# Hyperbolic attention: sums of ratio and root by accumulating DMAs that GpSimd issues, six pairs of heads instead of four through products

## The chip, the cores and the metric

The kernel runs on one NeuronCore of a Trainium2 chip. Its engines are TensorE (PE; its weight loads are shown apart as PEld), VectorE (DVE), ScalarE (ACT), GpSimd (POOL) and SyncE (SP), which run their own instruction streams in order and meet at semaphores, and 16 DMA engines. The metric is the device time of one execution in microseconds (us). A profiled execution is described by its span, from the first to the last instruction.

## The reference, cut to what matters

The program computes two transformer blocks on `x` of 32 x 256 x 128 (32 batches of 256 tokens of width 128, float32): causal attention, a mixture of experts, hyperbolic attention, and an MLP, each on a layer-normed input and with a residual. The change touches the third part alone:

```python
def _hyperbolic_distance(q, k, c):                      # c = 1, 16 heads of width 8
    q_norm_sq = jnp.sum(q * q, axis=-1, keepdims=True)
    k_norm_sq = jnp.sum(k * k, axis=-1)[..., None, :]
    qk = jnp.einsum('bhnd,bhmd->bhnm', q, k)
    diff_sq = q_norm_sq + k_norm_sq - 2.0 * qk
    denom = (1.0 - c * q_norm_sq) * (1.0 - c * k_norm_sq)
    denom = jnp.maximum(denom, 1e-06)
    cosh_arg = 1.0 + 2.0 * c * diff_sq / denom
    cosh_arg = jnp.maximum(cosh_arg, 1.0)
    return jnp.arccosh(cosh_arg)
...
attn = jax.nn.softmax(-dist, axis=-1)
out = jnp.einsum('bhnm,bhmd->bhnd', attn, v)
```

With s = cosh_arg - 1, the weight before normalising is exp(-arccosh(1+s)) = 1 / (1 + s + sqrt(s(s+2))). The same number is 1 / (sqrt(1+s/2) + sqrt(s/2))^2. The kernel uses the first form for some heads and the second for the others.

## The kernel before, in words

Four stages follow each other: `causal_attention`, `moe`, `hyperbolic_attention` (L1235 on) and `mlp`. The hyperbolic stage lies between about 1300 and 2425 us of the span. It works batch by batch (`b` = 0 to 31), and within a batch by 8 pairs of heads (`p` = 0 to 7). One pair is a tile of 128 partitions x 1024 float32 (two heads, two halves of 128 query rows, 256 keys), so 4 KB in each partition and 512 KB in all.

A pair of batch `b` goes this way:

- PE multiplies feature rows into `d_ps` and `i_ps` in PSUM (`pe_pairs`, L1353). There is one buffer of each, so the multiplies of the next pair wait until DVE has read `d_ps` (`dist_done`) and `i_ps` (`u_done`).
- DVE makes u = max(d, 0) (`dve_distances`, L1528) and then u = min(i, 1e6) * u (`dve_ratio`, L1532), the ratio s. `u` is a ring of 12 tiles (RING), and a slot is free again when PE has multiplied the weights that were in it with the values (`pv_done`).
- For the pairs in PRODUCTS (0, 1, 2, 3) GpSimd computes s(s+2) into one of six `spare` tiles (`pool_product`, three instructions, L1468, L1469, L1471). ACT takes one root of it in place (L1433). For the pairs 4 to 7 ACT takes two roots itself (`act_roots`): sqrt(1+s/2) into `spare` (L1438) and sqrt(s/2) in place in `u` (L1439).
- GpSimd adds `spare` to `u` (`pool_sum`, L1460).
- ACT takes the logarithm of the sum and the exponential of its multiple (`act_weights`, L1447 and L1450).
- PE multiplies the weights with the values (`pe_values`, L1369). Transposes, a normalisation on DVE (L1544, L1547), a projection and a residual follow.

The order on each engine is written out by hand. ACT does, in the loop body of batch `b`, the logarithms and exponentials of batch `b - 1`, and then the roots of batch `b`, with a load of its function table ahead of each of the two groups (L1654 and L1433). GpSimd does the products of batch `b` and then its eight sums, nothing else. DVE does ratios and distances of batch `b` with the row features of batch `b + 1` (`dve_features`, in the turn of pair 4), the copies of transposed rows (L1426), and the normalising of batch `b - 2` between them. PE follows the same pairs.

`spare` has six tiles (SPARE) for eight pairs: pair `p` uses tile `p % 6`. `spare_user` names who had the tile before: pair 6 of batch `b - 1` for pair 0, pair 7 of batch `b - 1` for pair 1, the same pair of batch `b - 1` for the pairs 2 to 5, and pairs 0 and 1 of the same batch for the pairs 6 and 7. Whoever writes `spare` waits until that sum is finished (`sum_done`).

Of the kernel before, what the change touches and what calls it, by code (L numbers as in the profile page):

```python
# [12 lines left out]
ALU = mybir.AluOpType  # L13
# [38 lines left out]
def after(engine, semaphore, count):  # L52

    if isinstance(count, int) and count <= 0:
        return
    engine.wait_ge(semaphore, count)
# [303 lines left out]
def causal_attention(nc, keep, batches):  # L360
# [12 lines left out]
    with ExitStack() as stack:  # L373
# [99 lines left out]
        def pe_turn(pe, p, s):  # L473
            k = p * SLOTS + s
            pe.wait_ge(exp_done, k + 1)
            wait_turned(pe, *at_lag(p, s, 2))
            for c in range(4):
                last = nc.tensor.transpose(t_ps[s % 2][:, c * P:(c + 1) * P], prob[:, s % 3, c, :], keep.ident)  # L478
            last.then_inc(p_turned, 1)

        def pe_values(pe, p, u, i):
            g, a = divmod(u, 2)
            wait_turned(pe, p, 3 * u)
            wait_turned(pe, p, 3 * u + 2)
            if a == 0:
                after(pe, o_copied, p * GROUPS + g)
                if g == 0:
                    pe.wait_ge(v_done, p + 1)
                    pe.wait_ge(v_cleared, 2)
            for q in range(GH):  # L490
                nc.tensor.matmul(o_ps[q * ROWS:(q + 1) * ROWS, a * N:(a + 1) * N], v[:, i, a * TB, g * GH + q, :],
                                 pT[:, u % 2, q, 0:2, :], start=True, stop=False, skip_group_check=True)
            for q in range(GH):
                last = nc.tensor.matmul(o_ps[q * ROWS:(q + 1) * ROWS, a * N + P:(a + 1) * N],
                                        v[:, i, a * TB + 1, g * GH + q, :], pT[:, u % 2, q, 2, :], start=False,
                                        stop=True, skip_group_check=True)
            last.then_inc(pv_done, 1)

        def pe_turn_back(pe, p, t, makes):
            pe.wait_ge(o_copied, (p + 1) * GROUPS)  # L500
            pe.wait_ge(v_done, makes)
            after(pe, attn_done, p * PT + t)
            for g in range(GROUPS):
                last = nc.tensor.transpose(misc[:, g * P:(g + 1) * P], o[:, t // TB, g, t % TB * P:(t % TB + 1) * P],
                                           keep.ident)
            last.then_inc(o_turned, 1)

        def pe_turn_attn(pe, p):
            pe.wait_ge(attn_done, (p + 1) * PT)
            for t in range(PT):  # L510
                last = nc.tensor.transpose(misc[:, t * P:(t + 1) * P], attn[:, t, :], keep.ident)
            last.then_inc(attn_turned, 1)
# [152 lines left out]

        END = pairs - 1

        with nc.Block() as block:
            @block.tensor
            def _(pe):  # L670
# [31 lines left out]
                for s in range(SLOTS - TURN_LAG, SLOTS):  # L702
                    pe_turn(pe, END, s)
                for u in range(UNITS - 2, UNITS):
                    pe_values(pe, END, u, 1)
                for t in range(PT):
                    pe_turn_back(pe, END, t, pairs)
                pe_turn_attn(pe, END)
                pe_project(pe, END)

# [527 lines left out]
def hyperbolic_attention(nc, keep, batches):  # L1238
# [3 lines left out]
    HP = H // 2  # L1242
# [5 lines left out]
    SPARE = 6  # L1248
    RING = 12
    TURN = 3  # L1250
    PRODUCTS = (0, 1, 2, 3)
    ROWS_BY_SCALAR = (0, 3)
    EARLY_ROWS = 5
    VALUES_AT = (2, 3, 4, 5)
# [1 line left out]
    with ExitStack() as stack:  # L1256
# [8 lines left out]
        u = m.sb("u", [P, RING, 2 * W2])  # L1265
        spare = m.sb("spare", [P, SPARE, 2 * W2])
# [21 lines left out]
        S_ = m.sem  # L1288
# [6 lines left out]
        inv_hi_done, rows_done, rows_turned, rowsT_done = S_("inv_hi_done"), S_("rows_done"), S_("rows_turned"), [S_(f"rowsT_done{n}") for n in range(2)]  # L1295
        pair_ready, dist_done, u_done = S_("pair_ready"), S_("dist_done"), S_("u_done")
        raised = S_("raised")
        prod_done, root_done, sum_done, ln_done, w_done, pv_done = S_("prod_done"), S_("root_done"), S_("sum_done3"), S_("ln_done"), S_("w_done"), S_("pv_done3")
        o_copied, o_turned, rec_done, attn_done = S_("o_copied3"), S_("o_turned3"), S_("rec_done3"), S_("attn_done3")
        attn_turned, attnT_done, proj_ready, res_done = S_("attn_turned3"), S_("attnT_done3"), S_("proj_ready3"), S_("res_done3")  # L1300

        def spare_user(b, p):

            return (b, p - SPARE) if p >= SPARE else (b - 1, p + SPARE if p + SPARE < HP else p)

        def slot(i, p):

            return (i * HP + p) % RING
# [120 lines left out]
        def act_roots(act, b, p, i):  # L1429
            pair, extra = u[:, slot(i, p), :], spare[:, p % SPARE, :]  # L1430
            if p in PRODUCTS:
                act.wait_ge(prod_done, b * len(PRODUCTS) + PRODUCTS.index(p) + 1)
                last = nc.scalar.activation(extra, extra, ACT.Sqrt)  # L1433
            else:
                act.wait_ge(u_done, b * HP + p + 1)
                before = spare_user(b, p)
                after(act, sum_done, before[0] * HP + before[1] + 1)
                nc.scalar.activation(extra, pair, ACT.Sqrt, bias=1.0, scale=0.5)  # L1438
                last = nc.scalar.activation(pair, pair, ACT.Sqrt, scale=0.5)  # L1439
            last.then_inc(root_done, 1)  # L1440

        def act_weights(act, b, p, i, logarithm):
            pair = u[:, slot(i, p), :]
            whole = p in PRODUCTS
            if logarithm:
                act.wait_ge(sum_done, b * HP + p + 1)
                nc.scalar.activation(pair, pair, ACT.Ln, bias=1.0 if whole else 0.0).then_inc(ln_done, 1)  # L1447
            else:
                act.wait_ge(ln_done, b * HP + p + 1)
                nc.scalar.activation(pair, pair, ACT.Exp, scale=-1.0 if whole else -2.0).then_inc(w_done, 1)  # L1450
# [6 lines left out]

        def pool_sum(pool, b, p, i):
            pool.wait_ge(root_done, b * HP + p + 1)
            nc.gpsimd.tensor_tensor(u[:, slot(i, p), :], u[:, slot(i, p), :], spare[:, p % SPARE, :], ALU.add).then_inc(sum_done, 1)  # L1460

        def pool_product(pool, b, p, i):
            pool.wait_ge(u_done, b * HP + p + 1)
            before = spare_user(b, p)
            after(pool, sum_done, before[0] * HP + before[1] + 1)
            n = b * len(PRODUCTS) + PRODUCTS.index(p)
            pair, extra = u[:, slot(i, p), :], spare[:, p % SPARE, :]
            nc.gpsimd.tensor_tensor(extra[:, 0:4], pair[:, 0:4], twos[:, :], ALU.add)  # L1468
            nc.gpsimd.tensor_scalar(extra[:, 4:2 * W2], pair[:, 4:2 * W2], 1.0, 2.0, ALU.mult, ALU.add).then_inc(raised, 1)  # L1469
            pool.wait_ge(raised, n + 1)  # L1470
            nc.gpsimd.tensor_tensor(extra, extra, pair, ALU.mult).then_inc(prod_done, 1)  # L1471
# [96 lines left out]
        def over_batches(engine, body):  # L1568


            def turn(r, some):
                for i in range(some):
                    b = TURN * r + i
                    known = isinstance(b, int)
                    body(b, i, not known or b >= 1, not known or b >= 2, not known or b >= 3, not known or b + 1 < batches,
                         not known or b + 2 < batches)
            whole = batches // TURN
            turn(0, TURN)
            with engine.Fori(1, whole) as r:
                turn(r, TURN)  # L1580
            turn(whole, batches % TURN)

        END = batches - 1

        with nc.Block() as block:
# [92 lines left out]
            @block.gpsimd  # L1678
            def _(pool):
                nc.gpsimd.memset(rows[:, :, :, :, :].bitcast(F32), 0.0).then_inc(v_cleared, 1)  # L1680
                nc.gpsimd.memset(v[:, :, :, :, DH:ROWS], 0.0).then_inc(v_cleared, 1)
                pool.wait_ge(v_cleared, 2)
                nc.gpsimd.memset(rows[:, 0, :, :, NORM_K:NORM_K + 2].bitcast(F32), 1.0).then_inc(zeroed, 1)
                nc.gpsimd.memset(rows[:, 1, :, :, NORM_Q:NORM_Q + 2].bitcast(F32), 1.0).then_inc(zeroed, 1)
                nc.gpsimd.memset(v[:, :, :, :, DH:VW], 1.0).then_inc(zeroed, 2)
                nc.gpsimd.memset(twos[:, :], 2.0).then_inc(v_cleared, 1)
                pool.wait_ge(v_cleared, 3)

                def body(b, i, one_before, two_before, three_before, one_after, two_after):
                    for p in PRODUCTS:  # L1690
                        pool_product(pool, b, p, i)
                    for p in range(HP):
                        pool_sum(pool, b, p, i)
                over_batches(pool, body)

            @block.vector
            def _(dve):
# [296 lines left out]
```

## Time and profile before

| | |
|---|---|
| median of 3 runs | 2583.7 us (2578.2 to 2590.47) |
| span of the profiled execution | 2563.6 us |
| median less span (what lies around the instructions) | 20.1 us |
| hyperbolic stage | about 1300 to 2425 us |
| PE, DVE, ACT, POOL busy over the span | 81%, 78%, 72%, 65% |

The shares over the whole span say little, because the four stages have different limits. Within the hyperbolic stage the work repeats once for each batch, so it is read as a period: the time between one event and the same event of the next batch. For an engine, busy time in a stretch, idle time before an instruction, and who ended that idle time are the three things to look for. An engine can be busy for nearly the whole period and still not set it, if the little idle time it has is a wait for somebody else. The time of an instruction is from its start to its end; back to back instructions overlap a little, so the distance from start to start is the pace.

### The profile page before, as it was taken

The page shows a single profiled execution, that of the slowest core. Times are in us where ns is not written, and L with a number is a line of the kernel's source. Part 1 is how long each engine was busy: PE and PEld are TensorE (multiplying, and loading weights), DVE is VectorE, ACT ScalarE, POOL GpSimd, SP SyncE. Part 2 cuts the span into 40 slices and gives each one's busy share as a digit, 9 for nine tenths or more (in the row PEclk, how much of TensorE's full clock was granted, in tenths as well). Part 3 has the DMA queues.
Part 4 walks back from the last instruction along what each step waited for, and adds up shares of the span by engine and source line. Part 5 has one row for each costly group of instructions (what it writes and reads, how often), then busy time and mean ns, then how long its engine had stood idle before and what let it go on. Part 6 is the DMA issues. An engine that isn't in the chain of part 4 may idle for free. (4 is left out here: it accounts for less than half of the span.)

```text
span 2563.6 us, 50172 instructions
## 1 busy us (share of the span) xinstructions
PE 2079.1 (81%) x14935; PEld 1515.9 (59%) x14935; DVE 1998.1 (78%) x6007; ACT 1854.7 (72%) x3188; POOL 1663.5 (65%) x1516
## 2 busy tenths in 40 slices
PE   4999999999999979999947666666666666666599
PEld 4777777777777668888834444443433444434266
DVE  4677777777777757877768999999999999999522
ACT  2666666666666634344239999999999999999743
POOL 2767766676667400000058999999999999999600
PEclk7999999999999969999966677777777777777599
DMA  5000000000000024334200000000000000000011
GB/s 136 1 2 2 1 1 0 1 0 1 1 0 1 2 67 108 93 92 110 68 1 1 1 1 0 0 0 0 0 0 0 0 0 0 0 0 1 7 31 37
DMA packets 44067, 49.03 MB, mean 19 GB/s; under 512 B 5112, under 2 KB 27038, under 8 KB 43934
## 3 DMA queue, kind: packets, MB, share of 16 engines
q1 hardware_dynamic: 35614, 43.32, 7.0%
q10 hardware_dynamic: 8320, 4.19, 0.7%
q8 instruction: 52, 0.85, 0.1%
q14 instruction: 81, 0.66, 0.1%
HBM read 42.78 MB, written 4.72 MB: 19 GB/s over the span
## 5 line engine op out<-in xcount | busy, mean ns | idle before, releaser
L1460 POOL TENSOR_TENSOR u<-u,spare 128x1024 f32<-128x1024 f32 x256 | 597.2, 2372 | 35.1 <-ACT spare L1433 34.9
L545 ACT ACTIVATE prob<-s_ps,nmax 128x128 f32<-128x128 f32 (+1 forms) x1024 | 364.4, 432 | 140.1 <-DVE nmax L602 140.0
L1353 PE MATMUL d_ps<-rowsT 28*128 28x256 f32 x1024 | 165.9, 404 | 331.3 <-DVE u L1532 331.2
L602 DVE CUSTOM_DVE_ANT_0 s_ps<-s_ps,mask 128x128 f32<-128x128 f32 (+1 forms) x1024 | 341.3, 385 | 101.8 <-issue 77.9
L1353 PEld LDWEIGHTS d_ps<-rowsT 28*128 28x128 f32 x1024 | 106.2, 242 | 430.4 <-issue 430.0
L582 POOL TENSOR_TENSOR g_lo<-g_all,g_hi 128x512 fp32r<-128x512 f32 x256 | 329.1, 1286 | 21.4
L1528 DVE TENSOR_SCALAR u<-d_ps 128x1024 f32<-128x1024 f32 x256 | 311.9, 1218 | 39.5 <-PE i_ps L1353 39.3
L1532 DVE SCALAR_TENSOR_TENSOR u<-i_ps,u 128x1024 f32<-128x1024 f32 x256 | 313.5, 1225 | 14.8
L1471 POOL TENSOR_TENSOR spare<-spare,u 128x1024 f32<-128x1024 f32 x128 | 303.1, 2368 | 10.7
L1447 ACT ACTIVATE u<-u 128x1024 f32<-128x1024 f32 x256 | 258.3, 1070 | 0.0
L1450 ACT ACTIVATE u<-u 128x1024 f32<-128x1024 f32 x256 | 257.5, 1066 | 0.0
L537 ACT COPY g_all<-g_ps 128x512 f32<-128x512 f32 x256 | 151.6, 592 | 126.9 <-PE g_ps L63 125.9
L994 POOL TENSOR_TENSOR x_lo<-xTs,x_hi 128x512 fp32r<-128x512 f32 x16 | 21.9, 1366 | 327.0 <-ACT x_hi L990 327.0
L1369 PE MATMUL o_ps<-u,v 128*32 128x256 f32 x2048 | 197.8, 522 | 43.1 <-ACT u L1450 43.0
L478 PE MATMUL t_ps<-ident,prob 128*128 128x128 f32 x1536 | 229.8, 272 | 1.6 <-ACT pT L612 1.2
L1341 PE MATMUL r_ps<-ident,rows 128*128 128x128 f32 x1024 | 217.9, 360 | 6.8 <-DVE rows L1523 6.1
L478 PEld LDWEIGHTS t_ps<-ident,prob 128*128 128x128 f32 x1536 | 190.6, 140 | 54.8 <-ACT prob L545 2.0
L1162 ACT ACTIVATE act_g<-eg_ps 128x512 f32<-128x512 f32 x128 | 76.3, 598 | 189.9 <-PE eg_ps L63 188.1
L1341 PEld LDWEIGHTS r_ps<-ident,rows 128*128 128x128 f32 x1024 | 163.9, 186 | 69.3 <-issue 53.5
L615 DVE COPY pT<-t_ps 128x512 f32<-128x512 f32 x256 | 176.7, 690 | 28.5 <-PE t_ps L478 22.6
L61 PE MATMUL s_ps<-g_hi,x_hi 128*128 128x512 f32 x384 | 185.9, 484 | 3.8 <-POOL g_lo L582 3.8
L558 POOL TENSOR_TENSOR g_hi<-g_all,ones 128x4 fp32r<-128x4 f32 x256 | 51.5, 201 | 194.6 <-ACT g_all L537 191.1
(265 smaller groups left out, 5577.9 us busy)
## 6 DMA issues: line engine op xcount, KB each, us to landing
w_all<-w_rows SPq DMA_DIRECT2D x128, 256.0 KB, 5.6
x<-L_attn_x ACTq DMA_DIRECT2D x8, 512.0 KB, 14.0
y<-y_rows SPq DMA_DIRECT2D x16, 256.0 KB, 2.3
wkqv<-L_attn_Wkqv SPq DMA_DIRECT2D x4, 528.0 KB, 8.7
gate_rows<-L_ffn_gate_proj SPq DMA_DIRECT2D x1, 512.0 KB, 14.5
up_rows<-L_ffn_up_proj SPq DMA_DIRECT2D x1, 512.0 KB, 11.5
down_cols<-L_ffn_down_proj SPq DMA_DIRECT2D x1, 512.0 KB, 13.3
w_rows<-wT SPq DMA_DIRECT2D x8, 64.0 KB, 1.6
```

The lines of the kernel that those rows point to most:

```text
L478: last = nc.tensor.transpose(t_ps[s % 2][:, c * P:(c + 1) * P], prob[:, s % 3, c, :], keep.ident)
L545: last = nc.scalar.activation(prob[:, kind, at, :].rearrange("p c n -> p (c n)"), s_ps[kind][:, at.start * P:at.stop * P], ACT.Exp, bias=n ...
L582: nc.gpsimd.tensor_tensor(g_lo[:, gb, q, :], g_all[:, h % 2, :], g_hi[:, gb, q, :], ALU.subtract).then_inc(g_split, 1)
L602: last = nc.vector.tensor_tensor_reduce(out=scores, in0=scores, in1=keep.mask[:, N - width:N], scale=-1.0, scalar=3.4e38, op0=ALU.add, op1 ...
L1341: last = nc.tensor.transpose(r_ps[p % 2][:, at:at + P], src, keep.ident)
L1353: last = nc.tensor.matmul(ps[:, e * W2 + j * N:e * W2 + (j + 1) * N], rowsT[at, slot(i, p), 1, j * P:(j + 1) * P], rowsT[at, slot(i, p), 0 ...
L1447: nc.scalar.activation(pair, pair, ACT.Ln, bias=1.0 if whole else 0.0).then_inc(ln_done, 1)
L1450: nc.scalar.activation(pair, pair, ACT.Exp, scale=-1.0 if whole else -2.0).then_inc(w_done, 1)
L1460: nc.gpsimd.tensor_tensor(u[:, slot(i, p), :], u[:, slot(i, p), :], spare[:, p % SPARE, :], ALU.add).then_inc(sum_done, 1)
L1471: nc.gpsimd.tensor_tensor(extra, extra, pair, ALU.mult).then_inc(prod_done, 1)
L1528: nc.vector.tensor_scalar(u[:, slot(i, p), :], d_ps[:, :], 0.0, None, ALU.max).then_inc(dist_done, 1)
L1532: nc.vector.scalar_tensor_tensor(out=u[:, slot(i, p), :], in0=i_ps[:, :], scalar=1.0 / DEN_MIN, in1=u[:, slot(i, p), :], op0=ALU.min, op1= ...
```

## The change

`pool_sum` no longer adds on GpSimd. It issues a DMA from `spare` to the pair's tile of `u` that adds to what is there (`accum_op=ALU.add`). Each of the six tiles of `spare` has a semaphore of its own (`sum_landed`) that this DMA raises by 16 when it has landed. Everybody who waited for `sum_done` now waits for it through `wait_sum`: ACT ahead of a logarithm, and ACT or GpSimd ahead of writing `spare`. PRODUCTS becomes (0, 1, 2, 3, 4, 5): the pairs 4 and 5 get three GpSimd instructions each, and ACT takes one root for them instead of two. The loop of GpSimd over the batches is written out, so that its waits are for constants, and it waits for the last eight sums at its end.

```diff
-    PRODUCTS = (0, 1, 2, 3)
+    PRODUCTS = (0, 1, 2, 3, 4, 5)
...
+        sum_landed = [S_(f"sum_landed{n}") for n in range(SPARE)]
...
+        def wait_sum(engine, b, p):
+
+            users = 2 if p % SPARE < HP - SPARE else 1
+            after(engine, sum_landed[p % SPARE], 16 * (users * b + p // SPARE + 1))
...
                 act.wait_ge(u_done, b * HP + p + 1)
-                before = spare_user(b, p)
-                after(act, sum_done, before[0] * HP + before[1] + 1)
+                wait_sum(act, *spare_user(b, p))
...
             if logarithm:
-                act.wait_ge(sum_done, b * HP + p + 1)
+                wait_sum(act, b, p)
...
         def pool_sum(pool, b, p, i):
             pool.wait_ge(root_done, b * HP + p + 1)
-            nc.gpsimd.tensor_tensor(u[:, slot(i, p), :], u[:, slot(i, p), :], spare[:, p % SPARE, :], ALU.add).then_inc(sum_done, 1)
+            nc.gpsimd.dma_start(u[:, slot(i, p), :], spare[:, p % SPARE, :], accum_op=ALU.add).then_inc(sum_landed[p % SPARE], 16)
 
         def pool_product(pool, b, p, i):
             pool.wait_ge(u_done, b * HP + p + 1)
-            before = spare_user(b, p)
-            after(pool, sum_done, before[0] * HP + before[1] + 1)
+            wait_sum(pool, *spare_user(b, p))
...
+        def written_out(body):
+
+            for b in range(batches):
+                body(b, b % TURN, b >= 1, b >= 2, b >= 3, b + 1 < batches, b + 2 < batches)
...
-                over_batches(pool, body)
+                written_out(body)
+                for p in range(HP):
+                    wait_sum(pool, END, p)
```

On GpSimd, at the boundary of batch 0 and batch 1, the kernel before has the last product of a batch, its eight sums, and the first product of the next batch in this order:

```order
L1468 TENSOR_TENSOR spare<-u,twos 128x4 [waits u_done]
L1469 TENSOR_SCALAR spare<-u 128x1020
L1471 TENSOR_TENSOR spare<-spare,u 128x1024 [waits raised]
L1460 TENSOR_TENSOR u<-u,spare 128x1024 [waits root_done] x8
L1468 TENSOR_TENSOR spare<-u,twos 128x4 [waits sum_done3,u_done]
```

The same place (last product of batch 1, its sums, first products of batch 2) in the changed kernel:

```order
L1472 TENSOR_TENSOR spare<-u,twos 128x4 [waits sum_landed5,u_done]
L1473 TENSOR_SCALAR spare<-u 128x1020
L1475 TENSOR_TENSOR spare<-spare,u 128x1024 [waits raised]
L1465 DMA u<-spare 128x1024 [waits root_done] x8
L1472 TENSOR_TENSOR spare<-u,twos 128x4 [waits sum_landed0,u_done]
L1473 TENSOR_SCALAR spare<-u 128x1020
L1475 TENSOR_TENSOR spare<-spare,u 128x1024 [waits raised]
L1472 TENSOR_TENSOR spare<-u,twos 128x4 [waits sum_landed1,u_done]
```

Eight sums are now eight issues, and the first products behind them wait for the landing of the sums of the pairs 6 (`sum_landed0`) and 7 (`sum_landed1`) of the batch ahead. The additions themselves have left the engine's stream, so its order no longer fulfils that wait.

On ACT, the roots of a batch stand in the kernel before behind the table load like this:

```order
L1433 ACT_TABLE_LOAD
L1433 ACTIVATE spare<-spare 128x1024 [waits prod_done] x4
L1438 ACTIVATE spare<-u 128x1024 [waits sum_done3,u_done]
L1439 ACTIVATE u<-u 128x1024
L1426 CAST rowsT<-r_ps 128x512 [waits pair_ready,rows_turned]
```

and in the changed kernel like this:

```order
L1439 ACT_TABLE_LOAD
L1439 ACTIVATE spare<-spare 128x1024 [waits prod_done] x5
L1432 CAST rowsT<-r_ps 128x512 [waits pair_ready,rows_turned]
L1439 ACTIVATE spare<-spare 128x1024 [waits prod_done]
L1443 ACTIVATE spare<-u 128x1024 [waits sum_landed0,u_done]
L1444 ACTIVATE u<-u 128x1024
L1443 ACTIVATE spare<-u 128x1024 [waits sum_landed1,u_done]
L1444 ACTIVATE u<-u 128x1024
```

Two of the four double roots have become single ones, and the two that remain (pairs 6 and 7) wait for the landing of the sums of the pairs 0 and 1 of the same batch.

## Rows read from the trace of the kernel before

**Rows 1.** Busy us of each engine by stretch, then PE clock, DMA share, GB/s.
```profile
core 0: us, PE busy (x) PEld busy (x) DVE busy (x) ACT busy (x) POOL busy (x), PEclk, DMA share, GB/s
1700.00:1800.00 100.00, 64.74 (x534) 40.50 (x538) 91.40 (x177) 97.47 (x125) 95.98 (x60) 0.72 0.00 0
```

**Rows 2.** Waits between 1500 and 2100 us: total us, times, longest us.
```profile
PE d_ps L1353 <- DVE u L1532: 186.3, 105, 4.9
PE o_ps L1369 <- ACT u L1450: 21.4, 18, 1.2
DVE rec L1544 <- PE misc L1380: 21.2, 18, 1.2
POOL u L1460 <- ACT spare L1433: 18.3, 18, 1.2
DVE u L1528 <- PE i_ps L1353: 17.5, 35, 0.5
ACT rows L1417 <- PE r_ps L1341: 13.6, 17, 0.9
```

**Rows 3.** Timeline of PE: start us, us, engine, line, operation [idle before <-releaser].
```profile
1739.07 1.07 PE L1369 MATMUL o_ps<-u,v 128*32 128x256 f32 x16 [1.23 <-ACT u L1450]
1740.08 0.83 PE L1380 MATMUL misc<-ident,o 128*128 128x128 f32 x4
1745.43 0.58 PE L1353 MATMUL d_ps<-rowsT 28*128 28x256 f32 x2 [4.52 <-DVE u L1532]
```

**Rows 4.** Timeline of ACT: the table load of batches five and thirty.
```profile
1484.26 1.28 ACT L1654 ACT_TABLE_LOAD   x1
...
2337.74 1.28 ACT L1654 ACT_TABLE_LOAD   x1
```

**Rows 5.** Timeline of ACT, the roots of a batch.
```profile
1709.33 1.28 ACT L1433 ACT_TABLE_LOAD   x1
1710.62 3.90 ACT L1433 ACTIVATE spare<-spare 128x1024 f32<-128x1024 f32 x4
1714.43 1.04 ACT L1438 ACTIVATE spare<-u 128x1024 f32<-128x1024 f32 x1
1715.38 1.04 ACT L1439 ACTIVATE u<-u 128x1024 f32<-128x1024 f32 x1
```

**Rows 6.** Timeline of POOL: a batch's last product, its sums, two products behind them.
```profile
1707.15 0.21 POOL L1468 TENSOR_TENSOR spare<-u,twos 128x4 f32<-128x4 f32 x1
...
1711.76 18.66 POOL L1460 TENSOR_TENSOR u<-u,spare 128x1024 f32<-128x1024 f32 x8 [0.97 <-ACT spare L1433]
1730.36 0.22 POOL L1468 TENSOR_TENSOR spare<-u,twos 128x4 f32<-128x4 f32 x1
...
1734.00 0.20 POOL L1468 TENSOR_TENSOR spare<-u,twos 128x4 f32<-128x4 f32 x1
```

**Rows 7.** Busy time by stretch, as in rows 1, where DMAs run.
```profile
10.00:12.00 2.00, 1.11 (x5) 1.11 (x6) 0.18 (x1) 0.00 (x0) 0.00 (x0) 1.00 1.11 332
950.00:1000.00 50.00, 50.00 (x314) 43.28 (x313) 39.45 (x109) 22.37 (x42) 2.60 (x2) 1.00 0.36 87
```

**Rows 8.** DMA issues: tile, queue, operation, times, KB each, median us to landing.
```profile
y<-y_rows SPq DMA_DIRECT2D x16, 256.0 KB, 2.3
w_rows<-wT SPq DMA_DIRECT2D x8, 64.0 KB, 1.6
```

**Rows 9.** Timeline of SyncE's queue: start us, us that one issue takes.
```profile
2449.48 0.39 SPq L1888 DMA_DIRECT2D y<-y_rows  x1
```

**Rows 10.** Timeline of POOL, the first batch: its first product and its first sum.
```profile
1316.44 0.20 POOL L1468 TENSOR_TENSOR spare<-u,twos 128x4 f32<-128x4 f32 x1 [17.83 <-DVE u L1532]
...
1330.84 18.59 POOL L1460 TENSOR_TENSOR u<-u,spare 128x1024 f32<-128x1024 f32 x8
```

**Rows 11.** Timeline of ACT, the last batch: its first root and its last logarithms.
```profile
2389.12 2.96 ACT L1433 ACTIVATE spare<-spare 128x1024 f32<-128x1024 f32 x3
...
2416.75 1.99 ACT L1447 ACTIVATE u<-u 128x1024 f32<-128x1024 f32 x2
```

More of the change, by code:

```diff
@@ L1297, in hyperbolic_attention @@
         raised = S_("raised")
-        prod_done, root_done, sum_done, ln_done, w_done, pv_done = S_("prod_done"), S_("root_done"), S_("sum_done3"), S_("ln_done"), S_("w_done"), S_("pv_done3")
+        prod_done, root_done, ln_done, w_done, pv_done = S_("prod_done"), S_("root_done"), S_("ln_done"), S_("w_done"), S_("pv_done3")
+        sum_landed = [S_(f"sum_landed{n}") for n in range(SPARE)]
         o_copied, o_turned, rec_done, attn_done = S_("o_copied3"), S_("o_turned3"), S_("rec_done3"), S_("attn_done3")
```

## The prediction

> **What bounds the kernel now.** I read the busy time by stretch first, then the waits, then the timelines. In a stretch of the hyperbolic stage the DMA share is 0.00 while ACT is busy 97%, POOL 96% and DVE 91% [rows 1]. By shares, ACT or POOL seem to set the pace, and the change relieves both. The waits say otherwise [rows 2]. The stretch of 600 us holds some 18 batches. POOL idles 1.0 us a batch, ahead of its first sum, for ACT. ACT idles 0.8 us a batch, for PE's transposes of feature rows. DVE idles for PE alone: 1.2 us a batch ahead of the normalising and twice 0.5 us ahead of a distance. No row has DVE waiting for ACT or POOL. PE waits for DVE, 10 us a batch. PE waits for ACT too, 1.2 us a batch, but that wait is covered: it stands at 1739.07, the work behind it is over at 1740.9, and then PE idles 4.52 us more until DVE frees the single PSUM buffers [rows 3]. So the period is a loop of DVE and PE, and ACT and POOL follow it with about 1 us to spare. The period is (2337.74 - 1484.26) / 25 = 34.14 us [rows 4].
>
> **What the change removes.** On POOL eight sums of 18.66 us in all [rows 6]. On ACT two of the eight L1438/L1439 roots of a batch, one start to start distance of 0.95 us each [rows 5], 1.9 us. Both engines only have slack before the loop of DVE and PE, so this takes nothing from the period. What is late next is what was late before: DVE.
>
> **What it adds on POOL.** A product costs the distance between two of them, 1734.00 - 1730.36 = 3.6 us [rows 6], so two more cost 7.2 and six cost 21.7. Then there are eight issues. The trace has no DMA issued by POOL. The nearest row is SyncE's issue, 0.39 us [rows 9]; the other end is the 2.33 us of the sum it replaces, since a reason to be dearer than the addition of 1024 elements is not in sight. I take 1.0, about the geometric mean of the two. POOL's own work is then 21.7 + 8.0 = 29.7 us of 34.14. POOL is not too busy.
>
> **What it adds in DMA.** Eight transfers of 512 KB per batch, where nothing moved. No row shows an accumulating DMA, so I bound its pace T. One pass over 524288 bytes at 332 GB/s, the best rate of a stretch [rows 7], is 1.58 us. But an addition has to read both `spare` and `u`, so twice that many bytes come in for each tile written: 3.16 us. A slower row is the copies of weights, 87 GB/s at a share of 0.36, so 242 GB/s if the engines were always busy [rows 7]; two reads at that pace are 4.33 us. I take 3.16: two reads are what the operation needs, and the 332 was reached with the engines saturated (share 1.11), as they will be here. For starting and completing I take the store of 64 KB, 1.6 us to landing less 0.2 for its bytes, and the one of 256 KB, 2.3 less 0.8 [rows 8]: 1.5 us, with 1.0 to 3 as bounds.
>
> The Trainium skill, Collectives: The Full Stack, section The bandwidth ceiling: the fold count and why AG ≠ RS ≠ AR, says of an adding DMA that it is slower than a copy because it reads two sources through one ring, not because of the add, with some 31 GB/s per DMA engine for the reading. The estimate from that page is 16 x 31 / 2 = 248 GB/s, T = 2.1; the period formed below would be 39.0 and the time about 2735. No row here shows an adding DMA.
>
> **The new wait, and the chain behind it.** GpSimd executes in order: products of a batch, issues of its sums, products of the next batch. The first two products of the next batch write the `spare` tiles of the pairs 6 and 7. They used to find these sums done, because POOL had just done them itself. Now POOL stands there until the DMAs have landed, and the four products behind them stand too. Those are waited for by ACT's roots, and the roots by the next issues. With E the end of a batch's sixth product, the loop is:
> - issue of the first sum: 1.0. Its root is long done, and the roots of the pairs 1 to 5 come at 0.95 us each or are done, faster than T. The roots of 6 and 7 wait for sums 0 and 1 to land, but are issued while sums 2 to 5 still move.
> - start and completion: 1.5.
> - seven sums until that of pair 6 has landed: 7 x 3.16 = 22.1. The sum of pair 7 lands during the first product, which is longer (3.6).
> - six products: 21.7.
>
> Sum: 46.3 us from E to E. It exceeds 34.14, so it becomes the period, and DVE, ACT and PE wait for it. For T over 3.6 the last sum decides instead: 2.5 + 8T + 18.1.
>
> **The sum.** In the first batch the products begin at 1316.44 [rows 10], so the sixth ends at 1316.44 + 21.7 = 1338.1. After 31 periods the sixth product of the last batch ends at 1338.1 + 31 x 46.3 = 2773.4. Eight sums land 1.0 + 1.5 + 25.3 = 27.8 later, at 2801.2, and the last logarithms start. Before, they start at 2416.75 [rows 11]. The rest behind them is unchanged, so the span grows by 384 us, from 2563.6 to 2948. That is the profiled execution's own measure; with the 20 us by which the median of the runs stands above it, it is 2968, my forecast. The PE clock, 0.72 here [rows 1], does not matter: PE is not in the chain. Nor is the logarithm of the pairs 4 and 5, which takes the other form at the same price.
>
> **The rivals.**
> *Two reads, but quicker.* The 332 GB/s came from loads of the inputs from HBM; here source and target are both tiles on the core, with rows of 4 KB. With T = 2.36, halfway between one pass and two, the period is 2.5 + 16.5 + 21.7 = 40.7, and the same steps give about 2790. Chance 0.25 for T between 1.6 and 2.7 (2620 to 2870).
> *Slower adding.* T of 4.33 gives 2.5 + 34.6 + 18.1 = 55.2, 653 us for 31 periods and some 20 more at the ends: 3257. T could be more if the adding limits. Chance 0.18 for T over 3.9 (over 3150).
> *One pass.* If reading the second operand costs nothing, T = 1.58: 2.5 + 11.1 + 21.7 = 35.3, so 1.1 x 31 = 35 us more, about 2620. With the cheap ends (issue 0.4, start and end 1.0) it is 34.2 and the loop of DVE and PE keeps the pace: 2584. Chance 0.07 together with the next one, 0.05 of it within 0.5%.
> *A plain copy's pace.* A quicker transfer, under 1.5, leaves POOL with slack and the change does nothing, 2584. The Trainium skill, DMA: Bandwidth & Descriptors, section Anatomy of one DMA, gives 2.0 us and bytes at 436 GB/s for a DMA from GpSimd, so 1.2 us a tile; its figures are for copies, and the estimate by it is a period of 1.0 + 2.0 + 8.4 + 21.7 = 33.1, no change. This trace never reaches that rate.
> *Faster.* If the 0.8 us that ACT waits a batch is an effect and ACT is what really closes the loop with PE (PE waits 1.2 us for its weights), then 1.9 us less on ACT shorten every period, provided T is under about 1.4, from where six products and eight landings fit into 32.2 us. It gives 2583.7 - 60 = 2524. Against it: 4.5 us of idle time behind that wait [rows 3]. Chance 0.05.
>
> **How the numbers follow.** Forecast (T of 2.7 to 3.9) 0.45, quicker 0.25, slower adding 0.18, one pass or copy's pace 0.07, faster 0.05. The range goes from 2600, just under one pass with its likely prices, to 3300, just over two reads at the slowest row; about 0.08 lies above and 0.10 below. Half a per cent (13 us) is about what can be told from no change. Faster by more: 0.05. Within: 0.05. Slower by more: 0.90.
>
> **What would show it.** In the changed profile POOL's first product of each batch (L1472) should be preceded by some 13 us of idle time (24.6 us from E to the landing of the sum of pair 6, less the 12 us until the last issue) that a DMA ended; DMAs should be busy over half of the period; ACT should wait ahead of the roots of pair 6 (L1443) and for the products (L1439). DVE's share should fall from 91% to some 67%. A table load should come every 46 us. I am wrong in T if landings are spaced otherwise than 3.16 us, in the cost of an issue if POOL's issues follow at more than 1 us, and in the whole chain if POOL doesn't idle. If the period is 34 with idle POOL, transfers are cheap; if it is 32, my reading of the loop is wrong.

## The result and the profile after

| | kernel before | changed kernel |
|---|---|---|
| median | 2587.1 us (4 runs) | 2856.8 us (4 runs) |
| span of the profiled execution | 2563.6 us | 2853.8 us |
| ratio of the times | | 1.101, 95% interval 1.096 to 1.106 |
| period of the hyperbolic stage, steady | 34.14 us | 42.5 us |

The change made the kernel 10% slower: 270 us where 384 were forecast. The forecast of 2968 us was 111 too high, and the mechanism was the one in the prediction. The kernel before ran between 2559 and 2597 us in the rounds of this case, with medians from 2573 to 2592; so each experiment below is compared, as a ratio, with the kernel before in its own round, and the times in us are not compared across rounds.

Of the 290 us between the two spans 23 have nothing to do with the change. They lie ahead of the hyperbolic stage, in code that is the same: its first row feature reciprocal comes at 1305.6 us before and at 1328.2 after, and executions of other kernels below differ there in the same way. So the stage is compared by itself. The same shift corrects a row of the table before: the 20.1 us of "median less span" do not lie around the instructions. In the runs whose time and span are both on record the time is some 2 us longer than the span (2855.75 and 2853.8 here). So most of the 20 is that the profiled execution of the kernel before was a quick one. The reciprocal of the row features runs once a batch; these are its rows in the trace of the kernel before, of the changed one, and of two experiments that are told below (times of first and last, of 32):

```profile
L1501 DVE RECIPROCAL r_ps<-sides x32: 950/954/961, 1305.6 to 2354.5; 128x128 f32<-128x128 f32 x32
```
```profile
L1505 DVE RECIPROCAL r_ps<-sides x32: 950/957/967, 1328.2 to 2625.9; 128x128 f32<-128x128 f32 x32
```
```profile
L1505 DVE RECIPROCAL r_ps<-sides x32: 951/958/966, 1304.3 to 2353.3; 128x128 f32<-128x128 f32 x32
```
```profile
L1505 DVE RECIPROCAL r_ps<-sides x32: 948/953/960, 1329.4 to 2327.3; 128x128 f32<-128x128 f32 x32
```

From the first to the last are 31 batches: 1048.9 us before and 1297.7 after, the third (spare8) 1049.0, the fourth (best) 997.9. A mean period below is this distance over 31: 33.84 before, 41.86 after. It is a little under the steady period, because the first batches have less to do.

The sums of a batch in the changed kernel, timeline of POOL (answers to [rows 6]):

```profile
1704.76 2.35 POOL L1475 TENSOR_TENSOR spare<-spare,u 128x1024 f32<-128x1024 f32 x1
1707.06 5.29 POOL L1465 DMA_DIRECT2D u<-spare  x6
1714.19 0.85 POOL L1465 DMA_DIRECT2D u<-spare  x1 [1.84 <-ACT u L1444]
1717.04 0.86 POOL L1465 DMA_DIRECT2D u<-spare  x1 [2.00 <-ACT u L1444]
1727.96 0.20 POOL L1472 TENSOR_TENSOR spare<-u,twos 128x4 f32<-128x4 f32 x1 [10.07 <-DMA u<-spare]
...
1749.56 5.32 POOL L1465 DMA_DIRECT2D u<-spare  x6
```

This is the whole chain in six rows. The last product ends at about 1707.1. Eight issues follow, the last two held by roots. Then POOL stands for 10.07 us until a DMA has landed, and only then come the six products, until 1749.56. The distance from one first issue to the next is 42.50 us.

The roots of the same batch, timeline of ACT (answers to [rows 5]):

```profile
1703.55 1.06 ACT L1439 ACTIVATE spare<-spare 128x1024 f32<-128x1024 f32 x1 [2.54 <-POOL spare L1475]
1707.15 1.06 ACT L1439 ACTIVATE spare<-spare 128x1024 f32<-128x1024 f32 x1 [2.06 <-POOL spare L1475]
1711.89 1.06 ACT L1443 ACTIVATE spare<-u 128x1024 f32<-128x1024 f32 x1 [3.43 <-DMA u<-spare]
1714.74 1.06 ACT L1443 ACTIVATE spare<-u 128x1024 f32<-128x1024 f32 x1 [0.85 <-DMA u<-spare]
```

ACT waits for products, and its roots of pair 6 and 7 wait for the landing of sums 0 and 1. The waits from 1600 to 2200 us, 14 batches (answers to [rows 2]):

```profile
POOL spare L1472 <- DMA u<-spare: 150.8, 15, 10.1
PE r_ps L1347 <- ACT rowsT L1432: 118.2, 28, 5.4
DVE rowsT L1432 <- PE r_ps L1347: 97.7, 56, 4.8
ACT spare L1439 <- POOL spare L1475: 88.9, 42, 2.5
ACT spare L1443 <- DMA u<-spare: 60.4, 28, 3.5
```

The last four are the effect passed on: ACT waits for POOL, PE for the copies that stand in ACT's stream behind its roots, and DVE for PE. No engine is near its limit any more:

```profile
core 0: us, PE busy (x) PEld busy (x) DVE busy (x) ACT busy (x) POOL busy (x), PEclk, DMA share, GB/s
1700.00:1800.00 100.00, 61.62 (x411) 37.78 (x409) 75.52 (x133) 69.59 (x88) 69.24 (x65) 0.57 0.52 97
```

### The profile page after: what moved, and what is told of

Read it like the earlier page. It is cut to its first block and busy times, and to the rows that moved or that the text cites. A ratio compares the mean times of both kernels' runs of the same rounds, so it can differ in the third digit from the quotient of the medians.

```text
span 2853.8 us, 50088 instructions
## 1 busy us (share of the span) xinstructions
PE 2185.3 (77%) x14935; PEld 1568.9 (55%) x14935; DVE 2033.4 (71%) x6007; ACT 1806.6 (63%) x3124; POOL 1512.9 (53%) x1708
## 5 line engine op out<-in xcount | busy, mean ns | idle before, releaser
L1347 PE MATMUL r_ps<-ident,rows 128*128 128x128 f32 x1024 | 259.1, 413 | 269.2 <-ACT rowsT L1432 263.2
L1475 POOL TENSOR_TENSOR spare<-spare,u 128x1024 f32<-128x1024 f32 x192 | 452.9, 2359 | 16.0
L1347 PEld LDWEIGHTS r_ps<-ident,rows 128*128 128x128 f32 x1024 | 190.1, 214 | 351.2 <-ACT rowsT L1432 284.6
L1359 PE MATMUL d_ps<-rowsT 28*128 28x256 f32 x1024 | 183.7, 447 | 214.3 <-DVE u L1536 214.0
L1439 ACT ACTIVATE spare<-spare 128x1024 f32<-128x1024 f32 x192 | 196.2, 1052 | 205.5 <-POOL spare L1475 205.1
L1536 DVE SCALAR_TENSOR_TENSOR u<-i_ps,u 128x1024 f32<-128x1024 f32 x256 | 313.5, 1225 | 14.8
L1465 POOL DMA_DIRECT2D u<-spare x256 | 225.0, 1481 | 124.9 <-ACT u L1444 124.9
L1432 DVE CAST rowsT<-r_ps 128x512 fp32r<-128x512 f32 x192 | 132.0, 689 | 218.5 <-PE r_ps L1347 218.5
L1455 ACT ACTIVATE u<-u 128x1024 f32<-128x1024 f32 x256 | 257.8, 1068 | 0.0
L1375 PE MATMUL o_ps<-u,v 128*32 128x256 f32 x2048 | 210.6, 550 | 39.0 <-ACT u L1455 38.9
L1472 POOL TENSOR_TENSOR spare<-u,twos 128x4 f32<-128x4 f32 x192 | 38.2, 199 | 333.6 <-DMA u<-spare 300.1
L1473 POOL TENSOR_SCALAR spare<-u 128x1020 f32<-128x1020 f32 x192 | 199.9, 1041 | 0.1
```

The costliest lines, as they stand in the source:

```text
L1347: last = nc.tensor.transpose(r_ps[p % 2][:, at:at + P], src, keep.ident)
L1359: last = nc.tensor.matmul(ps[:, e * W2 + j * N:e * W2 + (j + 1) * N], rowsT[at, slot(i, p), 1, j * P:(j + 1) * P], rowsT[at, slot(i, p), 0 ...
L1465: nc.gpsimd.dma_start(u[:, slot(i, p), :], spare[:, p % SPARE, :], accum_op=ALU.add).then_inc(sum_landed[p % SPARE], 16)
L1536: nc.vector.scalar_tensor_tensor(out=u[:, slot(i, p), :], in0=i_ps[:, :], scalar=1.0 / DEN_MIN, in1=u[:, slot(i, p), :], op0=ALU.min, op1= ...
```

## The experiments

**Eight tiles of spare.** Each pair has a tile of its own, so nobody waits for a landing that has just been issued. (Two semaphores of the stage are saved for it: one that nobody waited for is dropped, and two that follow each other on DVE share one.)

```diff
-    SPARE = 6
+    SPARE = 8
```

> Edit: eight spare tiles instead of six, so each pair has its own and the first products of a batch wait for sums that landed long ago; roots of pairs 6 and 7 wait for nothing new. The DMAs are as many and as large as in the changed kernel. My theory (the loss is the chain from the landing of the sums of pairs 6 and 7 over six products to the next issues): the chain is cut, the loop of DVE and PE keeps the pace again, period 34.1 us, time about 2584, the kernel before. Rival (the DMA traffic itself or GpSimd's issues slow the engines): the period stays near 42.5 us and the time near 2857. Rival (ACT or GpSimd set the pace before): with 1.9 us less on ACT and GpSimd relieved, the period falls to 32.3 us, time about 2525.

Measured: 2564.7 us, ratio to the kernel before 0.997 (0.993 to 1.002); mean period 33.84, the same as before. It moves as many bytes as the changed kernel, in less time. (The expected time, 2584, was the kernel before in the first round; in this round that kernel has 2573.1.) Busy time by stretch:

```profile
1700.00:1800.00 100.00, 64.73 (x519) 40.38 (x516) 91.77 (x178) 92.11 (x116) 82.45 (x76) 0.71 0.64 121
```

PE and DVE have the numbers of [rows 1], at a DMA share of 0.64. So the whole loss was the wait for landings inside the chain, not the traffic and not the issues. (Both waits are gone together: that of the products and that of the roots of the pairs 6 and 7.) The same run says what the relief is worth: ACT is at 92% instead of 97, POOL at 82 instead of 96, and the time does not move. This refutes the prediction's rival "faster", in which 1.9 us less on ACT would shorten the period.

**A copy instead of an addition.**

```diff
-            nc.gpsimd.dma_start(u[:, slot(i, p), :], spare[:, p % SPARE, :], accum_op=ALU.add)...
+            nc.gpsimd.dma_start(u[:, slot(i, p), :], spare[:, p % SPARE, :])...
```

> Edit: the DMAs copy spare over u instead of adding, so the sum is left out of the computation; everything else is as in the changed kernel. Theory (an added tile takes 2.7 us because two tiles are read for it): a landing every 1.35 us, chain 0.9 + 1.3 + 7 x 1.35 + 21.6 = 33.2 us, under the loop of DVE and PE, so period 34.1 us, time about 2584, share of busy DMA about halved per tile. Rival (the writing or the number of pieces sets the pace, whatever is read): 2.7 us a tile, period 42.5, time 2857.

Measured: 2582.0 us, ratio 1.002 (0.997 to 1.006); mean period 33.94.

```profile
1700.00:1800.00 100.00, 72.01 (x532) 43.87 (x524) 90.39 (x173) 91.39 (x116) 73.16 (x76) 0.63 0.33 126
```

126 GB/s at a share of 0.33 is 382 GB/s with all engines busy; adding, in spare8, it is 121 / 0.64 = 189. The factor is two. So a tile costs 1.37 us copied and 2.77 added by this reading. POOL's timeline has the copies a second way:

```profile
1710.06 3.21 POOL L1465 DMA_DIRECT2D u<-spare  x6
...
1721.41 0.19 POOL L1472 TENSOR_TENSOR spare<-u,twos 128x4 f32<-128x4 f32 x1 [3.36 <-DMA u<-spare]
```

From the first issue to the landing of the copy of pair 6 are 11.35 us. Less 0.53 for the issue and the 1.27 for start and completion that are worked out below for the adding DMA, seven copies took 9.55 us, 1.36 each, against 2.68 for an addition. The factor of two is what two tiles read instead of one would make. It isn't shown that the reading is the cause: an addition that costs as much as a copy would look the same here.

**Other order of the products.** Two products whose tiles are free come ahead of the two that wait.

```diff
-    PRODUCTS = (0, 1, 2, 3, 4, 5)
+    PRODUCTS = (2, 3, 0, 1, 4, 5)
```

> Edit: products in the order 2, 3, 0, 1, 4, 5, so two products whose spare tiles are free stand ahead of the two that wait for landings. Theory: two products leave the chain, 0.9 + 1.3 + 7 x 2.7 + 4 x 3.6 = 35.5 us, and the product of pair 5 must wait for its ratio from DVE, which allows 37.4 us: period 35.5 to 37.5, time 2625 to 2690. Rival (DMA traffic or GpSimd's own work sets the pace): no change against 2857, since work and traffic are the same.

Measured: 2698.8 us, ratio 1.050 (1.038 to 1.061); mean period 37.5. The work and the traffic are those of the changed kernel, only the order differs, and half of its loss is gone. What is late next shows in POOL's timeline at the first two products of a batch:

```profile
1723.71 0.20 POOL L1472 TENSOR_TENSOR spare<-u,twos 128x4 f32<-128x4 f32 x1 [4.79 <-DVE u L1536]
1727.80 0.20 POOL L1472 TENSOR_TENSOR spare<-u,twos 128x4 f32<-128x4 f32 x1 [0.43 <-DVE u L1536]
```

They are those of the pairs 2 and 3, and they wait for DVE's ratios and not for a DMA. The time came out 9 us above the 2625 to 2690 that were expected, and the ratios that hold it are those of the pairs 2 and 3 and not that of pair 5: a miss in the place, and a small one in the size. Why these ratios are late was not tested. The waits from 1600 to 2000 us point at the change's other wait, which this order leaves in:

```profile
ACT spare L1443 <- DMA u<-spare: 47.4, 22, 3.5
PE r_ps L1347 <- ACT rowsT L1432: 42.5, 11, 4.6
```

ACT's roots of the pairs 6 and 7 still wait for the landing of the sums 0 and 1, and PE's transposes wait for the copy that stands behind these roots in ACT's stream; DVE then waits for PE.

**Adding DMAs alone**, with four pairs through products.

```diff
-    PRODUCTS = (0, 1, 2, 3, 4, 5)
+    PRODUCTS = (0, 1, 2, 3)
```

> Edit: the changed kernel with four pairs through products, so the accumulating DMAs alone. Theory: chain 0.9 + 1.3 + 7 x 2.7 + 4 x 3.6 = 35.5 us, little over the loop of DVE and PE, period 35.5, time about 2584 + 31 x 1.4 = 2627. Rival (the DMAs cost the time by themselves): near 2857. Rival (the two more products alone cost it): 2584.

Measured: 2611.1 us, ratio 1.017 (1.007 to 1.026); mean period 35.0, steady 35.4. Two products less in the chain are 7.2 us less, 42.5 - 7.2 = 35.3.

**Six products alone**, the sums still on GpSimd: the kernel before with `PRODUCTS = (0, 1, 2, 3, 4, 5)`.

> Edit: the kernel before with six pairs through products, sums still added by GpSimd: the other part of the change alone. Theory: GpSimd's own work becomes 18.7 + 6 x 3.6 = 40.4 us a batch, with the wait for the first root some 41, so it sets the period: about 2584 + 31 x 6.5 = 2785, 8 percent slower. Rival (ACT sets the pace, so less work on ACT counts more): not slower than 2584. It also shows why the two parts come together.

Measured: 2782.4 us, ratio 1.075 (1.065 to 1.085); mean period 39.5. Each part alone is slower than the kernel before, the one by 1.7% (0.7 to 2.6) and the other by 7.5, and both together by 10.1. Here POOL is busy 99% of a stretch, and ACT waits for its products (waits from 1500 to 2000 us):

```profile
1700.00:1800.00 100.00, 63.28 (x464) 37.00 (x460) 84.40 (x162) 83.13 (x107) 98.75 (x65) 0.62 0.00 0
```
```profile
ACT spare L1433 <- POOL spare L1471: 84.3, 36, 2.5
```

In the changed kernel POOL stands and waits instead.

**Less work on ACT and POOL in the kernel before.**

```diff
-                nc.scalar.activation(extra, pair, ACT.Sqrt, bias=1.0, scale=0.5)
-                last = nc.scalar.activation(pair, pair, ACT.Sqrt, scale=0.5)
+                if p < 6:
+                    last = nc.scalar.activation(extra, pair, ACT.Sqrt, bias=1.0, scale=0.5)
+                else:
+                    nc.scalar.activation(extra, pair, ACT.Sqrt, bias=1.0, scale=0.5)
+                    last = nc.scalar.activation(pair, pair, ACT.Sqrt, scale=0.5)
...
-            nc.gpsimd.tensor_tensor(u[:, slot(i, p), :], u[:, slot(i, p), :], spare[:, p % SPARE, :], ALU.add)
+            nc.gpsimd.tensor_tensor(u[:, slot(i, p), 0:W2], u[:, slot(i, p), 0:W2], spare[:, p % SPARE, 0:W2], ALU.add)
```

> Edit: the kernel before, with ACT's second root of pairs 4 and 5 left out (1.9 us less on ACT a batch) and GpSimd's additions over half of the columns (some 9 us less on GpSimd a batch); the result is not the attention any more. No DMA is added. Theory (a loop of DVE and PE sets the period): it stays 34.1 us, time as before, within 0.5 percent, and ACT and GpSimd only idle more. Rival (ACT or GpSimd set the pace): the period falls by up to 1.9 us to 32.3, 60 us or 2.3 percent less time.

Measured: 2587.9 us, ratio 0.998 (0.994 to 1.003); mean period 33.94.

```profile
1700.00:1800.00 100.00, 71.72 (x531) 43.94 (x532) 90.38 (x176) 91.39 (x118) 69.20 (x59) 0.63 0.00 0
```

POOL falls from 96 to 69%, ACT from 97 to 91%, and nothing comes of it. Two engines at 96 and 97% were not the bound. That leaves DVE, at 91%, in a loop with PE. PE's granted clock is lower in this stretch than in [rows 1], 0.63 against 0.72, so by itself this run could hide a gain behind a slower PE. The run spare8 has the same relief of ACT at a clock of 0.71, and no gain either.

**Row features split.** The same loop is attacked directly: DVE has one block of some 5 us of row features in the turn of pair 4 ([rows 3] show PE idle for 4.5 us in it), and elsewhere it waits for PE. Half of the block moves to where it waits.

```diff
                             if p == 4:
                                 dve_features(dve, b + 1)
+                            if p == 5:
                                 dve_features_end(dve, b + 1)
```

> Edit: the kernel before, with the second half of DVE's row features moved from the turn of pair 4 to the turn of pair 5. No instruction more or less. Theory (loop of DVE and PE): the last ones stand in time in which DVE waited for PE, so the period falls by some 0.6 us to 33.5, 20 us or 0.8 percent less; it then meets ACT's own 33.4 us, so not more. Rival (ACT or GpSimd set the pace): no change.

Measured: 2576.8 us, ratio 0.9946 (0.9917 to 0.9975); mean period 33.38, 0.46 less. So 0.5% come from moving DVE's work, where taking 1.9 us from ACT gave nothing. It is a little less than the 0.8% expected. Busy time by stretch shows the next bound at once:

```profile
1700.00:1800.00 100.00, 74.09 (x540) 46.62 (x540) 95.61 (x177) 98.79 (x126) 97.56 (x60) 0.62 0.00 0
```

ACT has no room now, at 98.8%.

**And a copy moved from DVE to ACT**, in the kernel before with the split.

```diff
+                        if one_before and p == 4:
+                            dve_copy_o(act, b - 1, 0, (i - 1) % TURN, nc.scalar.copy)
...
-                        if one_before and p == 4:
-                            dve_copy_o(dve, b - 1, 0, (i - 1) % TURN)
```

> Edit: as split, and the first copy of the products with the values (0.67 us) moved from DVE to ACT, between the logarithms. ACT had 33.4 us of work a batch and gets 0.5 more, so theory: period 33.9, time about 0.3 percent under before, not faster than split, since here ACT has no room. Rival (DVE's work alone counts): period 32.9, 1.5 percent less than before.

Measured: 2577.7 us, ratio 0.994 (0.990 to 0.998); mean period 33.43. DVE has less to do and the period stays: ACT is the bound, busy 99.8%, and PE waits for it between 1500 and 2000 us:

```profile
1700.00:1800.00 100.00, 72.66 (x540) 43.05 (x532) 90.99 (x170) 99.83 (x128) 97.35 (x60) 0.67 0.00 0
```
```profile
PE r_ps L1341 <- ACT rowsT L1426: 44.5, 30, 2.4
PE o_ps L1369 <- ACT o L1538: 19.1, 14, 1.6
```

**All together.** The changed kernel with eight tiles, the split and the copy on ACT.

> Edit: the changed kernel (adding DMAs, six pairs through products) with eight spare tiles, the split row features and the copy moved to ACT. ACT now has 1.9 us of room for it. Theory: period 32.9, 31 x 1.25 = 39 us or 1.5 percent less than before, and so the room that the change makes is worth something once the landing is out of the chain and DVE is relieved. Rival (the DMAs' traffic or ACT's slack don't matter): as split or as spare8, at most 0.8 percent less.

Measured: 2539.0 us, ratio to the kernel before 0.980 (0.976 to 0.985); mean period 32.19, 1.65 less. It beats both kernels. The gain is larger than the 1.25 us a batch that were expected; what sets the period now, with ACT at 98% and DVE at 94%, was not tested.

```profile
1700.00:1800.00 100.00, 73.63 (x556) 44.31 (x560) 93.86 (x184) 97.89 (x129) 87.61 (x81) 0.67 0.70 132
```

**The same with four pairs through products.**

> Edit: as best, but with four pairs through products: adding DMAs, eight spare tiles, split row features, the copy on ACT, and ACT's 1.9 us of roots back. Theory: ACT's own work of 33.9 us a batch sets the period, as in split_o: time 0.6 percent or so under before. Rival (the eight tiles and GpSimd's relief are what made best faster, not the roots taken from ACT): as best, 2 percent under before.

Measured: 2575.6 us, ratio 0.994 (0.990 to 0.999); mean period 33.41, ACT at 99.8%:

```profile
1700.00:1800.00 100.00, 73.88 (x532) 44.13 (x524) 90.81 (x170) 99.84 (x129) 63.25 (x60) 0.66 0.67 126
```

So the idea of the change, roots taken from ACT at GpSimd's cost, is worth 1.2 us a batch, but only where ACT is the bound. The DMAs that add make room for it on GpSimd, which was busy for 99% of a longer period when it added itself (six_pool); best with the additions on GpSimd was not run.

| kernel | mean period, us | ratio to before |
|---|---|---|
| before | 33.84 | 1 |
| changed | 41.86 | 1.101 |
| six_pool | 39.53 | 1.075 |
| order | 37.52 | 1.050 |
| four | 35.03 | 1.017 |
| copy | 33.94 | 1.002 |
| light | 33.94 | 0.998 |
| spare8 | 33.84 | 0.997 |
| split | 33.38 | 0.995 |
| split_o | 33.43 | 0.994 |
| best_four | 33.41 | 0.994 |
| best | 32.19 | 0.980 |

## Why the prediction was right

**The time** lies in the range that was given, 2600 to 3300, but that range was wide enough for most outcomes and proves little. 2857 is not in the band of the forecast itself (T, the time of one adding DMA in a full queue, of 2.7 to 3.9). It lies at the upper end of the rival "two reads, but quicker" (2620 to 2870), which had a chance of 0.25 against 0.45. What speaks for the prediction are the waits and steps below.

**What bounds the kernel before: right.** The loop of DVE and PE was read from who waits for whom, against the busy shares. light and spare8 confirm it from two sides (nothing gained by 1.9 us less on ACT), split from the third. No experiment shortened PE's part of the loop, so that part rests on the waits of [rows 2].

**The chain: right.** Its steps, as forecast and as the trace of the changed kernel has them:

| step | forecast | measured | from |
|---|---|---|---|
| issue of one sum | 1.0 | 0.88 | six issues, 5.29 us |
| start and completion | 1.5 | 1.27 | below |
| seven sums | 7 x 3.16 = 22.1 | 7 x 2.68 = 18.8 | below |
| six products | 21.7 | 21.6 | 1727.96 to 1749.56 |
| period | 46.3 | 42.5 | |

The sum of pair 0 has landed at 1711.89 at the latest, when ACT's root of pair 6 starts, 4.83 us after the first issue. That of pair 6 has landed when the first product starts, 20.90 us after it. Six landings lie between: 16.07 / 6 = 2.68 us each. What is left of the 4.83 is 4.83 - 0.88 - 2.68 = 1.27. The waits appear where they were forecast: POOL 10.1 us ahead of the first product (13 forecast, the same error of T), ACT ahead of L1439 and of L1443.

**The size of T: the step that was off.** "Two reads are what the operation needs, and the 332 was reached with the engines saturated" took 332 GB/s from loads of the inputs. The factor of two was right, the rate was not: between tiles of the core the same engines read 2 x 524288 / 2.68 = 391 GB/s. That makes 7 x 0.48 = 3.4 us a batch of the 3.8 that were too many, and start and issue the rest. 3.8 x 31 = 118 us, and 384 - 118 = 266. Measured are 290 us between the spans, less the 23 ahead of the stage: 268. The rival "two reads, but quicker" had the better number for T, between 1.6 and 2.7. Its reason, that both tiles are on the core and the 332 came from HBM, fits the 382 GB/s of the copies, but no run separates it.

**The rule that was weighed.** The Trainium skill, Collectives: The Full Stack, section The bandwidth ceiling, says of the adding step of a ring collective that it reads two sources and so goes at half the rate of the copying one: the runs agree for these local DMAs, 189 against 382 GB/s. The estimate from its 31 GB/s per engine was 2.1 us a tile; here it is 2.68, or 391 / 16 = 24.4 GB/s read per engine. The formula of the Trainium skill, DMA: Bandwidth & Descriptors, section Anatomy of one DMA, makes 1.2 us of a tile's bytes. That is near the copy here (1.37), and under half of the addition (2.68).

**The share of DVE** was forecast at 67% and is 76. The shorter period accounts for 73 (91.4 x 34.14 / 42.5). The rest is that DVE is busy for some 32 us of a batch instead of 31.2, though its instructions are no longer (its ratio takes 1225 ns in both traces); what makes the difference stays open. **The ends** of the stage cost 7 us by the forecast; they are inside the 266 and were not measured by themselves.

**The 20 us** that were added for what lies above the span belong to the level of the kernel before and not to the change; they move the forecast and leave the 384 as they are.

## What to carry to other kernels

An engine at 97% need not be the bound. Here its last per cent were waits for others, and no wait of the longest loop ended with it; look for the engine that waits only for its own partner. When work goes from an engine to a DMA, the order of that engine's stream stops guaranteeing that the work is done: every buffer that was free "because we just did it" becomes a wait of a full transfer queue, and what is behind it in the stream waits too. Give such buffers one more generation (here two tiles, 8 KB a partition, took back the whole loss of 10%), and spend the room that a relief makes on the loop that is the bound, or it gives nothing.

## What the runs showed of the hardware

- An adding DMA from tile to tile, 128 rows of 4 KB, moves one tile every 2.68 us, a copying one every 1.36 to 1.37 (copy). Both with eight such transfers a batch queued from GpSimd.
- GpSimd is held for 0.88 us by the issue of an adding DMA and for 0.53 by a copying one (six issues in 3.21 us in the experiment copy). The addition that it replaces takes 2.33.
- DMAs at a share of 0.64, adding from tile to tile, slow DVE and ACT by nothing that shows: in spare8 DVE's ratio takes 1225 ns and ACT's exponential 1067, in the kernel before 1225 and 1068, and the mean period is 33.84 us in both.
